# Twelve buffers instead of eight for the gathered rows of the experts, requested nine experts ahead

## The chip, the cores and the metric

The kernel runs on one core of one Trainium2 chip. The metric is device time in microseconds (us) of one execution, as the median of several. The engines of the core are TensorE (PE; its weight loads are listed apart as PEld), VectorE (DVE), ScalarE (ACT), GpSimd (POOL) and SyncE (SP), which here only requests transfers. The transfers run on 16 DMA engines that all queues share.

## What is computed

Four layers in a row, each followed by a layer norm of the residual sum: RWKV attention, a gated feed-forward, latent attention, and a mixture of experts. There are 4096 tokens (16 sequences of 256) of width 256. The change lies in the last layer:

```python
# 32 experts, capacity C = ceil(1.25 * 4096 / 32) = 160 slots each, 4 experts per token
Xp = x[slots_token].reshape(E, C, d)                   # gathered rows, 160 x 256 per expert
G = jnp.einsum('ecd,edi->eci', Xp, W_gate)             # i = 128
U = jnp.einsum('ecd,edi->eci', Xp, W_up)
Y = jnp.einsum('eci,eid->ecd', jax.nn.silu(G) * U, W_down)
Yf = Y.reshape(EC, d) * slots_w[:, None]
out = jnp.zeros((T, d), x.dtype).at[slots_token].add(Yf)
shared = jax.nn.silu(x @ shared_gate.T) * (x @ shared_up.T) @ shared_down.T
x = _layernorm(x + out + shared)
```

## The kernel before

The first three layers and the routing fill the first 1779 us; the routing has left, in the DRAM tensor `slots`, 160 rows for each expert (256 values of the token, 32 weights, one index: 289 floats). `moe_phase` does the rest. Its first part is a loop over the 32 experts, its second part (the tail) reads the sums back, adds them, norms them and stores the output. The engines run their own instruction streams and meet only at semaphores.

One expert e passes these steps:

- **Rows.** SP requests the 160 rows of e from `slots` into `e_rows[:, e % 8]` (`load_slots`, L2714; 80 partitions, two halves). This buffer is read three times: PE transposes it (`expert_turn`, L3095), ACT takes the slot weights out of it while it copies the result (`copy_y`, L2862), and POOL's additions take the indices out of it. So a buffer is free only when the additions of the expert that held it have landed.
- **Weights.** SP requests the three weight matrices of e (`load_w`, L2707) into a ring of seven. It waits until the weights seven experts back have been used by DVE and PE.
- **Matrix work.** PE transposes the rows two experts ahead (L3095), multiplies by gate and up one expert ahead (`expert_in`, L3109), and multiplies by down for e itself (`expert_out`, L3120). ACT and DVE stand between these steps.
- **Additions.** POOL issues two indirect DMAs for e (`add_rows`, L2776), one for each half of 80 rows, that add the result rows in DRAM. Even experts add into `sums0`, odd ones into `sums1`. Two experts that add into the same tensor may not overlap, so POOL first waits until the additions of e - 2 have landed (`y_added`). Result rows lie in `y_rows`, a ring of eight, which the change leaves as it is.

SP's stream in the loop is, for e = 0 to 31: every fourth expert one tile of `x_rows` for the shared part (`load_x`, L2701), then the weights of e + 7, then the rows of e + 7. The wait in front of these rows is on the additions of e - 1. SP stops at a wait, so whatever stands behind it waits too. The waits of `load_slots`, as they stand before:

```python
if e >= RING:
    sp.wait_ge(e_turned, e - RING + 1)
    for a in range(2):
        sp.wait_ge(y_added[e % RING][a], 16 * (e // RING))
```

Between the experts' steps PE, ACT and DVE also do the shared part for seven tiles of 256 tokens, and three more tiles after the loop. The tail starts with SP's wait for all additions (L2752), after which it requests the sums (L2747).

Of the kernel before, what the change touches and what calls it, by code (L numbers as in the profile page):

```python
# [644 lines left out]
E = 32  # L645
CAP = -(-5 * TOKENS // (4 * E))
CH2 = CAP // 2
SLOTROWS = E * CAP
ROW = D + E + 1
# [1925 lines left out]


RING = 8
WRING = 3
SUMRING = 6
STORE_LAG = SUMRING + 4  # L2580
# [11 lines left out]
def moe_phase(nc, w_experts, x3, slots_dram, sums_dram, out, ident, q_rows, wq_high, raw_kept, first_slots):  # L2592
    with ExitStack() as ctx:
        s = Scope(nc, ctx, "moe")

        def both(name, shape):
            return [s.sb(name + "_high", shape, F32R), s.sb(name + "_low", shape, F32R)]
# [6 lines left out]
        h_part = both("h", [P, SC, UNIT])  # L2604
        total = s.sb("total", [P, UT * LATE, D])
        wd_part = both("wd", [P, WRING, D])
        e_rows = s.sb("e_rows", [CH2, RING, 2, ROW])
        e_cols = s.sb("e_cols", [P, 2, KD, CAP])
        e_gate = s.sb("e_gate", [P, 2, CAP])
        e_hidden = s.sb("e_hidden", [P, 2, CAP])  # L2610
        eh_part = both("eh", [P, 2, CAP])
        y_rows = s.sb("y_rows", [CH2, RING, 2, D])
        y_in = s.sb("y_in", [P, SUMRING, SUMS, UT, D])
# [30 lines left out]
        raw_in = [s.sem(f"raw_in{r}") for r in range(WRAW)]  # L2644
        w_high = s.sem("w_high_done")
        w_low = s.sem("w_low_done")
        slots_in = [s.sem(f"slots_in{r}") for r in range(RING)]
        e_turned = s.sem("e_turned")
        e_copied = s.sem("e_copied")
        e_gate_ready = s.sem("e_gate_ready")  # L2650
# [6 lines left out]
        y_copied = s.sem("y_copied")  # L2657
        y_added = [[s.sem(f"y_added{r}_{a}") for a in range(2)] for r in range(RING)]
        sums_in = [s.sem(f"sums_in{r}") for r in range(SUMRING)]
# [14 lines left out]

        def slot_rows(e):

            return first_slots[:, :, :] if e == 0 else e_rows[:, e % RING, :, :]

        def wait_slots(eng, e):

            if e > 0:
                eng.wait_ge(slots_in[e % RING], 16 * (e // RING + (0 if e % RING == 0 else 1)))

        def unit_of(e):

# [11 lines left out]
        def _(sp):  # L2697
            def load_x(u):
                if u >= XRING:
                    sp.wait_ge(total_done, u - XRING + 1)  # L2700
                sp.dma_start(x_rows[:, u % XRING, :, :], unit_rows(x3, EARLY + u)).then_inc(rows_in[u % XRING], 16)  # L2701
# [5 lines left out]
                sp.dma_start(kept_raw(q_rows, raw_kept, e), w_experts[e]).then_inc(raw_in[e % WRAW], 16)  # L2707

            def load_slots(e):
                if e >= RING:  # L2710
                    sp.wait_ge(e_turned, e - RING + 1)
                    for a in range(2):
                        sp.wait_ge(y_added[e % RING][a], 16 * (e // RING))
                sp.dma_start(slot_rows(e),  # L2714
                             slots_dram[e * CAP:(e + 1) * CAP, :].rearrange("(a p) d -> p a d", p=CH2))\
                    .then_inc(slots_in[e % RING], 16)

            load_slots(1)
            load_x(0)
# [10 lines left out]
            load_slots(7)  # L2730
            load_x(2)
            load_x(3)

            for e in range(E):
                u, piece = unit_of(e)
                if piece == 0 and u >= 1 and u - 1 + XRING < LATE:
                    load_x(u - 1 + XRING)
                if e + WRAW < E:
                    load_w(e + WRAW)
                if e >= 1 and e - 1 + RING < E:  # L2740
                    load_slots(e - 1 + RING)

            def load_sums(p):
                if p >= SUMRING:
# [63 lines left out]
        def _(act):  # L2808
# [20 lines left out]
            def weights_high(e):  # L2829
                wait_raw(act, e)  # L2830
                if e >= WRING:
                    act.wait_ge(y_ready, e - WRING + 1)
                nc.scalar.activation(wd_part[0][:, e % WRING, :], kept_raw(q_rows, raw_kept, e)[:, EIN:], ACT.Copy)\
                    .then_inc(w_high, 1)
# [86 lines left out]
        def _(dve):  # L2921
# [24 lines left out]
            def weights_low(e):  # L2946
                dve.wait_ge(w_high, e + 1)
                nc.vector.tensor_tensor(wd_part[1][:, e % WRING, :], kept_raw(q_rows, raw_kept, e)[:, EIN:],
                                        wd_part[0][:, e % WRING, :].bitcast(F32), ALU.subtract).then_inc(w_low, 1)

# [339 lines left out]
```

## Time and profile before

| | us |
|---|---|
| median of 3 runs (1964.30 to 1968.96) | 1964.71 |
| the profiled execution's own time | 1963.74 |
| its span (first to last instruction) | 1961.8 |
| start of the expert loop's first additions | 1787.46 |
| last addition issued | 1912.55 |

All starts are microseconds from the start of the span. The profile names the releaser of an idle engine by the semaphore event that came last before the engine went on; where an instruction waits for several semaphores this can be another one than the one that really held it. The issue of an indirect DMA is an instruction on POOL of about 1.4 us; its transfers end later, and the trace shows that end as the moment at which a waiter goes on.

### The profile page before, as it was taken

What the parts mean: (1) busy time and instruction counts of PE and PEld (TensorE: products, weight loads), DVE (VectorE), ACT (ScalarE), POOL (GpSimd) and SP (SyncE); (2) the same over time, 40 slices, a digit from 0 to 9 for tenths busy, and PEclk for the clock granted to TensorE, in tenths of its full rate; (3) what the DMA queues carried; (4) which work ended last, traced back from release to release, by engine and by line L of the source; (5) the groups of instructions that cost most, each with busy time, mean ns of one, the idle gap of its engine ahead of it and who ended that gap; (6) DMA issues with size and microseconds to landing.
All of it is one profiled execution on the core that took longest, in us unless ns stands there. A gap on an engine that the chain in (4) does not pass through costs nothing. (4 is left out here: it accounts for less than half of the span.)

```text
span 1961.8 us, 35601 instructions
## 1 busy us (share of the span) xinstructions
PE 1833.9 (93%) x12032; PEld 1643.8 (84%) x12032; DVE 1483.0 (76%) x4074; ACT 1039.5 (53%) x2694; POOL 836.0 (43%) x863
## 2 busy tenths in 40 slices
PE   7999999999999999999999999999999999978880
PEld 6788888888888887888789999999999999977870
DVE  7978787787878796656677888888888888863436
ACT  5434343333333333333477777777777777735653
POOL 1232323232323220000244566666666666754776
PEclk9999999999999999999999999999999999988995
DMA  3201010000101003473200010000000000127867
GB/s 121 95 1 33 1 33 23 12 22 12 33 1 50 30 22 120 139 264 127 93 12 18 21 41 26 22 21 20 19 19 20 19 19 14 40 75 186 198 141 260
DMA packets 102003, 118.81 MB, mean 61 GB/s; under 512 B 12567, under 2 KB 93723, under 8 KB 101184
## 3 DMA queue, kind: packets, MB, share of 16 engines
q1 hardware_dynamic: 89104, 108.42, 17.0%
q0 software_dynamic: 12288, 8.11, 2.7%
q8 instruction: 98, 1.61, 0.4%
q14 instruction: 81, 0.66, 0.1%
q10 hardware_dynamic: 432, 0.02, 0.0%
HBM read 75.50 MB, written 57.10 MB: 68 GB/s over the span
## 5 line engine op out<-in xcount | busy, mean ns | idle before, releaser
L282 POOL TENSOR_TENSOR kept_q_rows<-kept_q_rows 128x512 f32<-128x512 f32 x128 | 203.5, 1590 | 527.3 <-DVE kept_q_rows L547 527.3
L1716 POOL TENSOR_TENSOR kept_raw<-kept_raw,mla_row_inv 128x512 f32<-128x512 f32 x192 | 199.2, 1038 | 258.4 <-DVE mla_row_inv L2056 257.2
L372 ACT ACTIVATE kept_q_rows<-rwkv_r 128x512 f32<-128x512 f32 x128 | 76.6, 599 | 399.3 <-DVE rwkv_o_low L468 396.7
L1874 ACT ACTIVATE kept_raw<-kept_raw,mla_least 128x256 f32<-128x256 f32 (+1 forms) x512 | 227.7, 446 | 74.2 <-DVE mla_least L2040 71.7
L2040 DVE CUSTOM_DVE_ANT_0 kept_raw<-mla_score,kept_mask 128x256 f32<-128x256 f32 (+1 forms) x512 | 157.1, 352 | 82.7 <-PE mla_score L2412 52.5
L532 DVE TENSOR_TENSOR kept_q_rows<-rwkv_v,kept_q_rows 128x512 f32<-128x512 f32 x128 | 88.1, 688 | 113.2 <-PE rwkv_v L583 110.9
L539 DVE TENSOR_TENSOR_SCAN rwkv_state<-rwkv_decay_w,kept_q_rows 128x256 f32<-128x256 f32 x256 | 166.0, 691 | 4.1
L1799 POOL DMA_INDIRECT slots<-mla_x_out,mla_slot_now x128 | 130.6, 1020 | 30.8 <-issue 23.2
L1890 ACT ACTIVATE mla_p_high<-mla_turn 128x512 fp32r<-128x512 f32 x192 | 114.0, 594 | 48.1 <-PE mla_turn L2420 46.5
L2050 DVE TENSOR_TENSOR mla_p_low<-mla_turn,mla_p_high 128x512 fp32r<-128x512 f32 x192 | 128.1, 667 | 2.1 <-ACT mla_p_high L1890 2.1
L2420 PE MATMUL mla_turn<-kept_ident,kept_raw 128*128 128x128 f32 x768 | 116.1, 274 | 8.5 <-DVE mla_p_low L2050 8.5
L2439 PE MATMUL mla_o<-mla_p_high,mla_v_high 128*128 128x256 f32 x384 | 117.9, 307 | 0.7 <-DVE mla_o_low L2061 0.4
L2420 PEld LDWEIGHTS mla_turn<-kept_ident,kept_raw 128*128 128x128 f32 x768 | 92.0, 141 | 29.9 <-issue 15.3
L2439 PE MATMUL mla_o<-mla_p_high,mla_v_low 128*128 128x256 f32 x384 | 108.7, 283 | 0.0
L2439 PE MATMUL mla_o<-mla_p_low,mla_v_high 128*128 128x256 f32 x384 | 108.3, 282 | 0.0
L600 PE MATMUL rwkv_out<-rwkv_w_high,rwkv_o_high 128*128 128x256 f32 x352 | 98.8, 281 | 4.8 <-DVE rwkv_o_low L468 4.8
L2776 POOL DMA_INDIRECT sums<-moe_y_rows,moe_e_rows x62 | 88.3, 1424 | 34.9 <-issue 14.3
L2375 PE MATMUL mla_proj<-kept_wq_high,kept_cq_high 128*128 128x512 f32 x240 | 99.0, 412 | 2.2 <-ACT kept_q_rows L1852 1.1
L932 ACT ACTIVATE ffn_gate<-ffn_gate,kept_scale_hid 128x512 f32<-128x512 f32 (+1 forms) x48 | 33.0, 688 | 126.3 <-PE ffn_gate L1164 126.3
L547 DVE SCALAR_TENSOR_TENSOR kept_q_rows<-kept_q_rows,rwkv_bonus_u,rwkv_state 128x512 f32<-128x512 f32 x128 | 96.3, 752 | 4.5
L600 PE MATMUL rwkv_out<-rwkv_w_high,rwkv_o_low 128*128 128x256 f32 x352 | 99.3, 282 | 0.0
L600 PE MATMUL rwkv_out<-rwkv_w_low,rwkv_o_high 128*128 128x256 f32 x352 | 98.6, 280 | 0.0
(505 smaller groups left out, 6265.6 us busy)
## 6 DMA issues: line engine op xcount, KB each, us to landing
kept_raw<-in_experts SPq DMA_DIRECT2D x27, 384.0 KB
kept_raw<-in_rkvo SPq DMA_DIRECT2D x16, 512.0 KB
moe_y_in<-sums SPq DMA_DIRECT2D x32, 256.0 KB, 4.7
sums<-ffn_empty SPq DMA_DIRECT2D x12, 512.0 KB
slots<-ffn_empty SPq DMA_DIRECT2D x16, 361.2 KB
moe_e_rows<-slots SPq DMA_DIRECT2D x31, 180.6 KB
kept_x_in<-x SPq DMA_DIRECT2D x18, 256.0 KB, 17.0
mla_x_res<-x SPq DMA_DIRECT2D x17, 256.0 KB
```

The source lines that it names most:

```text
L282: nc.gpsimd.tensor_tensor(gate[:, c % 2, :], key[:, c % 2, :], gate[:, c % 2, :], ALU.mult).then_inc(gated_done, 1)
L539: last_scan = nc.vector.tensor_tensor_scan(out=state[:, q, 1:SEQ + 1], data0=decay_w[:, c:c + 1].to_broadcast([P, SEQ]), data1=kv[:, q * S ...
L600: last = nc.tensor.matmul(out_ps[j // 2][:, (j % 2) * D:(j % 2 + 1) * D], o_part[op][:, c % 2, j * P:(j + 1) * P], w_chunk(wp, c)[:, 3 * D ...
L1716: nc.gpsimd.tensor_tensor(unit, unit, row_inv[:, v % PR, 0:len(heads)].rearrange("p (h a) -> p h a", a=1) .to_broadcast([P, len(heads), ke ...
L1799: nc.gpsimd.indirect_dma_start(slots_dram, bass.IndirectOffsetOnAxis(slot_now[:, of % 2, i:i + 1], 0), x_out[:, of % 2, i // TOPK, :], Non ...
L1874: last = nc.scalar.activation(probs[:, v % PR, i * keys:(i + 1) * keys], masked[:, v % 2, i * keys:(i + 1) * keys], ACT.Exp, bias=least[:, ...
L1890: nc.scalar.activation(p_part[0][:, v % PR, :], turn_ps[n % TURN_BANKS][:, :], ACT.Copy)\
L2040: last = nc.vector.tensor_tensor_reduce(out=masked[:, v % 2, i * keys:(i + 1) * keys], in0=score_ps[v % 2][:, i * keys:(i + 1) * keys], in ...
L2050: nc.vector.tensor_tensor(p_part[1][:, v % PR, :], turn_ps[n % TURN_BANKS][:, :], p_part[0][:, v % PR, :].bitcast(F32), ALU.subtract).then ...
L2375: last = nc.tensor.matmul(ps[:, :], cp, wp, start=(i == 0), stop=(i == 4))
L2420: last = nc.tensor.transpose(ps[:, i * P:(i + 1) * P], probs[:, v % PR, i * P:(i + 1) * P], ident[:, :])
L2439: last = nc.tensor.matmul(out, v_part[vp][:, seq % 2, kb, b, :], probs_t, start=(i == 0), stop=(i == len(terms) - 1))
```

## The change

The rows get twelve buffers (`SRING`) instead of eight, which takes 27.7 KB of a partition instead of 18.5 KB. SP requests the rows of expert 8 ahead of the loop, and in iteration e of the loop the rows of e + 9 (`SRING - SLACK`) instead of e + 7. The buffer of e + 9 is that of e - 3, so the wait in front of the request is on the transposition and the additions of e - 3, where it was on those of e - 1. The weights stay seven ahead, `y_rows` and the semaphores of the additions stay a ring of eight.

```diff
 RING = 8
+SRING = 12
+SLACK = 3
...
-        e_rows = s.sb("e_rows", [CH2, RING, 2, ROW])
+        e_rows = s.sb("e_rows", [CH2, SRING, 2, ROW])
...
-        slots_in = [s.sem(f"slots_in{r}") for r in range(RING)]
+        slots_in = [s.sem(f"slots_in{r}") for r in range(SRING)]
...
-            return first_slots[:, :, :] if e == 0 else e_rows[:, e % RING, :, :]
+            return first_slots[:, :, :] if e == 0 else e_rows[:, e % SRING, :, :]
...
-                eng.wait_ge(slots_in[e % RING], 16 * (e // RING + (0 if e % RING == 0 else 1)))
+                eng.wait_ge(slots_in[e % SRING], 16 * (e // SRING + (0 if e % SRING == 0 else 1)))
...
             def load_slots(e):
-                if e >= RING:
-                    sp.wait_ge(e_turned, e - RING + 1)
+                if e >= SRING:
+                    sp.wait_ge(e_turned, e - SRING + 1)
                     for a in range(2):
-                        sp.wait_ge(y_added[e % RING][a], 16 * (e // RING))
+                        sp.wait_ge(y_added[(e - SRING) % RING][a], 16 * ((e - SRING) // RING + 1))
...
             load_x(2)
             load_x(3)
+            load_slots(8)
...
-                if e >= 1 and e - 1 + RING < E:
-                    load_slots(e - 1 + RING)
+                if 8 <= e + SRING - SLACK < E:
+                    load_slots(e + SRING - SLACK)
```

No instruction is added or taken away on any engine; only SP's stream has another order. At the start of the expert loop SP's stream before was (rows of 6, weights of 6, rows of 7, two tiles of x, weights of 7 and 8, rows of 8, weights of 9):

```order
L2714 DMA moe_e_rows<-slots 80x2x289
L2707 DMA kept_raw<-in_experts 128x768
L2714 DMA moe_e_rows<-slots 80x2x289
L2701 DMA moe_x_rows<-x3 128x2x256 x2
L2707 DMA kept_q_rows<-in_experts 128x768
L2707 DMA kept_raw<-in_experts 128x768
L2714 DMA moe_e_rows<-slots 80x2x289
L2707 DMA kept_raw<-in_experts 128x768
```

and is now (rows of 6, weights of 6, rows of 7, two tiles of x, rows of 8, weights of 7, rows of 9, weights of 8, rows of 10, weights of 9):

```order
L2716 DMA moe_e_rows<-slots 80x2x289
L2709 DMA kept_raw<-in_experts 128x768
L2716 DMA moe_e_rows<-slots 80x2x289
L2703 DMA moe_x_rows<-x3 128x2x256 x2
L2716 DMA moe_e_rows<-slots 80x2x289
L2709 DMA kept_q_rows<-in_experts 128x768
L2716 DMA moe_e_rows<-slots 80x2x289
L2709 DMA kept_raw<-in_experts 128x768
L2716 DMA moe_e_rows<-slots 80x2x289
L2709 DMA kept_raw<-in_experts 128x768
```

The rows of 8 stood behind the weights of 8 and behind a wait; now the rows of 8, 9, 10 and 11 have no wait on additions at all, and the first such wait (on expert 0) stands in front of the rows of 12.

At the end of the loop SP's stream before was (rows of 29, weights of 30, rows of 30, last tile of x, weights of 31, rows of 31, then the first read of the sums):

```order
L2714 DMA moe_e_rows<-slots 80x2x289
L2707 DMA kept_raw<-in_experts 128x768
L2714 DMA moe_e_rows<-slots 80x2x289
L2701 DMA moe_x_rows<-x3 128x2x256
L2707 DMA kept_raw<-in_experts 128x768
L2714 DMA moe_e_rows<-slots 80x2x289
L2747 DMA moe_y_in<-sums0 128x2x256
```

and is now (rows of 30, weights of 29, rows of 31, weights of 30, last tile of x, weights of 31, then the first read of the sums):

```order
L2716 DMA moe_e_rows<-slots 80x2x289
L2709 DMA kept_raw<-in_experts 128x768
L2716 DMA moe_e_rows<-slots 80x2x289
L2709 DMA kept_raw<-in_experts 128x768
L2703 DMA moe_x_rows<-x3 128x2x256
L2709 DMA kept_raw<-in_experts 128x768
L2750 DMA moe_y_in<-sums0 128x2x256
```

The last request with a wait on additions was for the rows of 31 (on expert 23); now it is again for the rows of 31, but on expert 19, and nothing behind it waits for additions until the sums are read.

## Rows read from the trace of the kernel before

**Rows 1.** The page: the chain that ended last, its shares by engine

```profile
DMA 3%; PE 2%; issue 2%; DVE 1%; POOL 1%; ACT 0%; POOLq 0%; ACTq 0%; DVEq 0%; SPq 0%
```

**Rows 2.** Stretches: us, busy us by engine, clock, DMA share, GB/s

```profile
1780.00:1800.00 20.00, 19.37 (x147) 18.77 (x147) 8.62 (x22) 12.59 (x35) 7.53 (x6) 0.87 0.98 274
1794.00:1796.00 2.00, 2.00 (x19) 2.00 (x18) 1.58 (x4) 1.28 (x5) 1.41 (x1) 1.00 1.12 336
```

**Rows 3.** POOL in order of time: start, us, [idle before, releaser]

```profile
1789.30 1.44 POOL L2776 DMA_INDIRECT sums<-moe_y_rows,kept_first_slots  x1 [0.30 <-issue]
1794.42 1.41 POOL L2776 DMA_INDIRECT sums<-moe_y_rows,moe_e_rows  x1 [3.68 <-ACT moe_y_rows L2862]
1802.96 1.39 POOL L2776 DMA_INDIRECT sums<-moe_y_rows,moe_e_rows  x1 [1.91 <-ACT moe_y_rows L2862]
1811.57 1.39 POOL L2776 DMA_INDIRECT sums<-moe_y_rows,moe_e_rows  x1 [2.11 <-DMA sums<-moe_y_rows,moe_e_rows]
1828.11 1.40 POOL L2776 DMA_INDIRECT sums<-moe_y_rows,moe_e_rows  x1 [2.18 <-DMA sums<-moe_y_rows,moe_e_rows]
1844.30 1.40 POOL L2776 DMA_INDIRECT sums<-moe_y_rows,moe_e_rows  x1 [1.41 <-DMA sums<-moe_y_rows,moe_e_rows]
1873.71 1.55 POOL L2776 DMA_INDIRECT sums<-moe_y_rows,moe_e_rows  x1 [0.30 <-issue]
1886.59 1.40 POOL L2776 DMA_INDIRECT sums<-moe_y_rows,moe_e_rows  x1 [0.91 <-ACT moe_y_rows L2862]
1889.99 1.40 POOL L2776 DMA_INDIRECT sums<-moe_y_rows,moe_e_rows  x1 [0.30 <-issue]
1912.55 1.40 POOL L2776 DMA_INDIRECT sums<-moe_y_rows,moe_e_rows  x1 [0.30 <-issue]
```

**Rows 4.** ACT in order of time: the copy of expert 3's result

```profile
1798.45 0.83 ACT L2862 ACTIVATE moe_y_rows<-moe_y,moe_e_rows 80x256 f32<-80x256 f32 x2
```

**Rows 5.** The chain that ended last, in order of time: start, us, what

```profile
1804.66 6.05 DMA sums<-moe_y_rows,moe_e_rows
1891.69 3.18 DMA sums<-moe_y_rows,moe_e_rows
```

**Rows 6.** SP's requests in order of time: start, us, line, what

```profile
1796.71 0.33 SPq L2714 DMA_DIRECT2D moe_e_rows<-slots  x1
1802.18 0.33 SPq L2714 DMA_DIRECT2D moe_e_rows<-slots  x1
1810.79 0.32 SPq L2714 DMA_DIRECT2D moe_e_rows<-slots  x1
1811.70 0.37 SPq L2714 DMA_DIRECT2D moe_e_rows<-slots  x1
1871.28 0.32 SPq L2714 DMA_DIRECT2D moe_e_rows<-slots  x1
1887.55 0.32 SPq L2714 DMA_DIRECT2D moe_e_rows<-slots  x1
1915.81 2.42 SPq L2747 DMA_DIRECT2D moe_y_in<-sums  x5
```

**Rows 7.** Who waited for whom: us in total, times, longest us

```profile
SPq L2713 <- DMA sums<-moe_y_rows,moe_e_rows: 61.2, 13, 6.4
PEld moe_et L3095 <- DMA moe_e_rows<-slots: 13.3, 12, 2.1
```

**Rows 8.** PE in order of time: transpositions of the rows of experts 6, 14, 31

```profile
1798.26 0.44 PE L3095 MATMUL moe_et<-kept_ident,moe_e_rows 80*128 80x80 f32 x4
1824.46 0.44 PE L3095 MATMUL moe_et<-kept_ident,moe_e_rows 80*128 80x80 f32 x4
1892.03 0.50 PE L3095 MATMUL moe_et<-kept_ident,moe_e_rows 80*128 80x80 f32 x4 [0.94 <-DMA moe_e_rows<-slots]
```

**Rows 9.** Size of one request: out<-in, queue, count, KB

```profile
kept_raw<-in_experts SPq DMA_DIRECT2D x27, 384.0 KB
moe_e_rows<-slots SPq DMA_DIRECT2D x31, 180.6 KB
```

More of the change, by code:

```diff
@@ L2709, in load_slots @@
             def load_slots(e):
-                if e >= RING:
-                    sp.wait_ge(e_turned, e - RING + 1)
+                if e >= SRING:
+                    sp.wait_ge(e_turned, e - SRING + 1)
                     for a in range(2):
-                        sp.wait_ge(y_added[e % RING][a], 16 * (e // RING))
+                        sp.wait_ge(y_added[(e - SRING) % RING][a], 16 * ((e - SRING) // RING + 1))
                 sp.dma_start(slot_rows(e),
                              slots_dram[e * CAP:(e + 1) * CAP, :].rearrange("(a p) d -> p a d", p=CH2))\
-                    .then_inc(slots_in[e % RING], 16)
+                    .then_inc(slots_in[e % SRING], 16)
             load_slots(1)
```

## The prediction, made before the kernel was run

> **What bounds the kernel now.** I read four views, in this order. First the chain of waits that ended last, where DMA has the largest share [rows 1]: in the stretch that the change touches it runs through the indirect additions, their issue on POOL and their landing. Its pieces show an addition that takes 6.05 us from the start of its issue to its landing in the middle of the loop, and 3.18 us near its end [rows 5]. Second the timeline of POOL [rows 3]. Two halves make an expert, so in the loop the rows shown are the first half of expert 1 (1794.42), 3 (1802.96), 5 (1811.57), 9 (1828.11), 13 (1844.30), 21 (1873.71), 24 (1886.59) and 25 (1889.99), and the second half of 0 (1789.30) and of 31 (1912.55). Where POOL has no wait, an issue takes 1.40 us and the gap behind it 0.30 us, so the floor is 1.70 us for a half and 3.40 us for an expert. From the first half of expert 3 to the second half of expert 31 there are 57 steps: 57 x 1.70 = 96.9 us, and the trace shows 1912.55 - 1802.96 = 109.6 us. So 12.7 us of this stretch are waits, and this is all that a change in the loop can give back on this chain, since the tail starts with the landing of the last addition (SP's read of the sums at 1915.81 [rows 6], 3.26 us after 1912.55).
>
> What are these waits? The view names DMA for some and ACT's copy for others [rows 3]. I take the landing of the addition two experts back for all of them from expert 3 on. For expert 3, ACT has finished its copy at 1798.45 + 0.83 = 1799.28 [rows 4], 3.7 us before POOL goes on. And SP, which waits for the additions of expert 1 in front of the rows of expert 9, goes on at 1802.18 [rows 6], 0.78 us before POOL. At expert 5 the same distance stands again: SP at 1810.79 on the landing of expert 3, POOL at 1811.57, again 0.78 us [rows 3, 6]. One landing releases both.
>
> Third, SP's requests [rows 6] and the views of waits [rows 7]. SP waits 61.2 us for additions in front of rows (L2713, 13 times), and PE waits for rows 12 times, 13.3 us by its weight loads. PE's own pace shows how much that is: between the transpositions for experts 6 and 14 there are eight iterations in 26.20 us, 3.275 us each, without a wait; from 14 to 31 there are seventeen in 67.57 us, where 17 x 3.275 = 55.7 us would do. PE loses 11.9 us to late rows [rows 8]. Fourth, the stretches: the DMA engines are busy 0.98 of the time from 1780 to 1800 [rows 2].
>
> **What the change does to PE.** No instruction goes or comes. Rows of expert k + 8 were requested when the additions of k landed; now rows of k + 12. SP's next request, the weights, stands behind that wait: it was k + 9, now k + 11. Rows are used two iterations ahead of their expert, so they come four iterations, some 13 us, earlier than they did, against a longest wait of 2.1 us [rows 7, 8]. So PE's 11.9 us go. What is late next for PE is nothing until its lead over POOL grows: it then meets the weights, that still follow additions, and the eight buffers of `y_rows`. Is it worth anything for the end? POOL needs a result at least 3.40 us after the last one, and from expert 3 on no wait of POOL was for a result. PE earlier is cover on top of cover. I count 0 us.
>
> **What it does to the additions.** This decides, and it has three places.
>
> (a) *The start.* Rows of 8 to 11 and weights 9 and 10 now go out before the landing of expert 0 at about 1796.7, when they did not: 4 x 180.6 + 2 x 384 = 1490 KB [rows 9], at 274 GB/s [rows 2] an estimate of 5.6 us of DMA time, put into a stretch in which the engines are full (share 1.12 in 1794 to 1796 [rows 2]). Expert 0's second half, issued among the first requests, took 1796.7 - 1789.3 = 7.4 us to land; expert 1's, issued at about 1794.42 + 1.70 = 1796.1 when the queue was shorter, 6.0 us [rows 3, 6]. Now expert 1 has the long queue too: between 6.0 and 7.4 us, so expert 3 starts 0 to 1.4 us later. A gain is excluded, as no load is taken away ahead of it. The value lies between two rows that are alike near, and I take the middle, +0.7 us. The weights of 7 and 8 move behind one and two requests of rows (0.7 to 1.3 us each way at that rate), but are used five iterations later: 0.
>
> The Trainium skill (DMA: Bandwidth & Descriptors, section on queues, rings and completion order) states that each DMA engine goes round-robin between the queues it has work for, a packet at a time. By that rule the length of SP's queue would not matter to an addition so long as it is not empty, term (a) would be 0 and the sum 0.7 us lower. The two landings, 7.4 and 6.0 us, both with full engines, differ, so the trace doesn't quite bear it out; the queue's other contents differ too, so it doesn't refute it either.
>
> (b) *The middle.* Here lies the point of the whole change: SP still waits for an addition in every iteration, only for an older one. Is that wait still last? The weights of k + 11 need PE's work on k + 4. Expert 3 lands at 1810.7 while PE has transposed for expert 9 at about 1798.26 + 3 x 3.275 = 1808.1, so it has finished the gate and up work of 7; and PE only gets further ahead. So every landing still lets out one request of rows and one of weights, 565 KB [rows 9], about 2 us at 274 GB/s, at the very moment at which POOL issues the next addition. Two experts that land within 1 us (SP at 1810.79 and again at 1811.70) still let out a double load. The pace in fours of experts has been 16.5, 16.2 and 14.7 us (5 to 9, 9 to 13, and the mean of the two from 13 to 21) [rows 3], against a floor of 13.6 us; this pattern is one of POOL, SP and the DMA engines, and all three see the same bytes in the same order, shifted. The x tile moves from the landing of experts 2, 6, 10 to that of 4, 8, 12: same size, same frequency. I count 0, with bounds from the paces seen: sixteen experts at 14.7 throughout would give -(62.1 - 58.8) = -3.3 us, at 16.5 throughout +3.9 us.
>
> (c) *The end.* Before, the last request goes out at 1887.55 on the landing of expert 23, and from expert 25 on the pace is the floor [rows 3, 6]. Now the last one hangs on expert 19, whose landing is at about 1871.2 [rows 6]. Four experts fewer issue among loads. The least it gives is the wait of expert 24, 0.91 - 0.30 = 0.6 us. The average of waits is 12.7 us over the 22 experts 3 to 24, 0.58 each, so four are worth 2.3 us. Against that, the landing of 19 lets out rows, two weights and a tile of x at once, that is more than the pair before. I take half, -1.2 us, bounds -0.6 and -2.3.
>
> **The sum.** +0.7 + 0 + 0 - 1.2 = -0.5 us on the profiled execution of 1963.74 us: 1963.2 us. The median of the runs shown is 1964.71 us, 1.0 us above it, so the forecast for the median is 1964.2 us. The measurement of this kernel can tell about 0.3%, 5.9 us, from no change; this is within it.
>
> **Rivals.**
> - *Late results do hold POOL.* If the view's label is right where it names ACT's copy, and the chain really passes PE's late rows, PE's 11.9 us come off the end, bounded by POOL's 12.7 us: 1964.7 - 11.9 = 1952.8 us. For it: PE waits 12 times and the chain does contain rows. Against it: the two times of 0.78 us and the copy that was long done. The Trainium skill (DMA: Bandwidth & Descriptors, rules for kernel authors) advises to issue a DMA early and wait on its semaphore late; that rule would promise this rival, and for PE the trace agrees with it, but PE is not what ends last. Chance 0.07.
> - *The bursts fall apart.* If, with SP less tight, requests spread between additions, the middle runs at 14.7 us per four experts (-3.3 us) and the end gives its full 2.3 us, with (a) at 0: 1964.7 - 5.6 = 1959.1 us; at a still better pace of 14.2 another 2 us, 1957. For it: the pace did improve to 14.7 by itself from expert 13 on. Against it: SP's release by landings stays. Chance 0.25, and in a little over half of it the gain is over 5.9 us.
> - *Slower: the early backlog and the worst lock.* If the loads put ahead keep additions at 7.4 us past expert 3 (1.4 us at expert 3, the same again at expert 5) and the pace then locks at 16.5 us for all sixteen experts (+3.9 us), without a gain at the end, it is +6.7 us: 1971.4 us. It decides from the point at which a landing takes 1.35 us longer than the 6.05 us of now. For it: DMA share 0.98 at the start. Against it: these loads then aren't there later. Chance 0.10.
> - *The change doesn't do what it says*, rows come no earlier, since SP's wait is still on additions: then PE still loses its 11.9 us, and the time is the same, 1964.7 us. Since even this gives no change, it lies in the forecast's band. Chance 0.03.
>
> **How the numbers follow.** The forecast, within 4 us of 1964.2, has 0.55; 0.07, 0.25, 0.10 and 0.03 stand above. Over 0.3% faster: 0.07 + 0.14 = 0.21, to which I add 0.03 for gains of the forecast's own mechanism beyond its bounds: 0.24. Slower: 0.10 + 0.02 = 0.12. Within: 0.64. The range reaches down to 1957.0 us, which takes in the fallen bursts and leaves out late results, and up to 1970.0 us, the sum of the upper bounds (+1.4 + 3.9 - 0.6 = 4.7 us, 1969.4 us) and a little of the slower rival.
>
> **What would show it.** In the profile of the changed kernel PE's waits for rows should be nearly gone and its transposition for expert 31 well before 1885; SP should still wait for additions for tens of us at L2715; POOL should hold 10 to 14 us of waits between expert 3 and 31, with landings of about 6 us that follow SP's bursts; from about expert 23 on its pace should be 3.40 us. I am wrong in (b) if fours of experts take under 14.3 us or over 16.5 us on the mean, in (a) if expert 3 starts outside 1802.9 to 1804.5, and wrong about the bound if POOL starts within 1 us after a copy of ACT's again and again.

## The result and the profile after

The changed kernel takes 1969.17 us (median of 20 runs) where the kernel before takes 1964.76 us (20 runs beside them). The ratio is 1.0021 with a 95% interval of 1.0014 to 1.0028: it is 2.8 to 5.5 us slower. In two further comparisons the ratio was 1.0021 (1.0010 to 1.0031) and 1.0014 (1.0005 to 1.0023). The forecast was 0.5 us faster, 1964.2 us. The time lies in the forecast's range, but it moved the other way, and clear of the scatter.

The profiled execution has a span of 1969.0 us. First what the change was made for: the waits of PE and SP in the changed kernel (engine, line waited for, us in total, times, longest).

```profile
PEld moe_et L3098 <- DMA moe_e_rows<-slots: 0.7, 1, 0.7
POOL sums L2779 <- DMA sums<-moe_y_rows,moe_e_rows: 19.8, 16, 3.2
SPq L2715 <- DMA sums<-moe_y_rows,moe_e_rows: 46.3, 15, 6.4
```

PE's 12 waits for rows [rows 7] have become one. SP still waits for additions in front of the rows (46.3 us, 15 times), and POOL waits for them too. PE's timeline in the changed kernel shows the transposition for expert 31:

```profile
1884.28 0.50 PE L3098 MATMUL moe_et<-kept_ident,moe_e_rows 80*128 80x80 f32 x4 [0.49 <-DMA moe_e_rows<-slots]
1930.45 0.80 PE L3086 MATMUL moe_down_ps<-kept_wq_high,moe_h_high 128*128 128x256 f32 x2 [21.63 <-DVE moe_h_low L2940]
```

SP's first request of the last layer came at 1782.97 here and at 1779.44 before. Counted from it, PE is at expert 31 after 101.3 us where it was there after 112.6 us [rows 8]: 11.3 us earlier. What it gained it idles away later: the wait that ends at 1930.45 is 21.63 us long, and in the kernel before the same instruction waited 10.26 us, 11.4 us less:

```profile
1922.67 0.80 PE L3083 MATMUL moe_down_ps<-kept_wq_high,moe_h_high 128*128 128x256 f32 x2 [10.26 <-DVE moe_h_low L2937]
```

The next two fences show POOL and then SP in order of time in the changed kernel, as [rows 3] and [rows 6] do for before.

```profile
1799.72 1.40 POOL L2779 DMA_INDIRECT sums<-moe_y_rows,moe_e_rows  x1 [0.30 <-issue]
...
1807.86 1.39 POOL L2779 DMA_INDIRECT sums<-moe_y_rows,moe_e_rows  x1 [3.22 <-DMA sums<-moe_y_rows,moe_e_rows]
1809.56 1.75 POOL L2779 DMA_INDIRECT sums<-moe_y_rows,moe_e_rows  x1 [0.30 <-issue]
...
1816.95 1.42 POOL L2779 DMA_INDIRECT sums<-moe_y_rows,moe_e_rows  x1 [2.24 <-DMA sums<-moe_y_rows,moe_e_rows]
...
1882.36 1.40 POOL L2779 DMA_INDIRECT sums<-moe_y_rows,moe_e_rows  x1 [2.27 <-DMA sums<-moe_y_rows,moe_e_rows]
...
1890.47 1.39 POOL L2779 DMA_INDIRECT sums<-moe_y_rows,moe_e_rows  x1 [1.45 <-DMA sums<-moe_y_rows,moe_e_rows]
...
1919.37 1.40 POOL L2779 DMA_INDIRECT sums<-moe_y_rows,moe_e_rows  x1 [0.30 <-issue]
```

```profile
1782.97 0.32 SPq L2716 DMA_DIRECT2D moe_e_rows<-slots  x1
...
1807.08 0.31 SPq L2716 DMA_DIRECT2D moe_e_rows<-slots  x1
...
1816.17 0.32 SPq L2716 DMA_DIRECT2D moe_e_rows<-slots  x1
...
1882.96 0.42 SPq L2709 DMA_DIRECT2D kept_raw<-in_experts  x1
1922.65 2.42 SPq L2750 DMA_DIRECT2D moe_y_in<-sums  x5
```

Read them so. Expert 1's second half is issued at 1799.72; its landing lets SP go on at 1807.08 and POOL, with expert 3, 0.78 us later at 1807.86. That landing took 7.4 us, where it had taken 6.0 us. Expert 3's second half, issued at 1809.56, lands at 1816.1, after 6.6 us, and POOL starts expert 5 at 1816.95, again 0.78 us behind SP. The last row with a wait is that of expert 23 (1890.47); from there POOL runs at its floor.

The stretches of both kernels (us, busy us by engine, clock, DMA share, GB/s) show the loads that moved, first of the kernel before:

```profile
1800.00:1820.00 20.00, 20.00 (x173) 20.00 (x172) 9.84 (x24) 14.54 (x40) 13.36 (x10) 1.00 0.80 186
1880.00:1900.00 20.00, 16.25 (x133) 15.33 (x132) 7.11 (x19) 13.04 (x36) 15.93 (x12) 1.00 0.72 149
```

and of the changed one:

```profile
1800.00:1820.00 20.00, 20.00 (x173) 20.00 (x172) 9.21 (x23) 15.51 (x44) 12.61 (x9) 1.00 0.99 265
1880.00:1900.00 20.00, 14.46 (x107) 12.60 (x105) 6.18 (x15) 9.69 (x29) 13.85 (x11) 1.00 0.56 104
```

The DMA engines are now full from 1800 to 1820, and emptier than before at the end. The changed profile's last layer begins 3.5 us later, so the two stretches don't hold quite the same work. Counted from SP's first request they say the same in all profiles of the two kernels (three of before, four of the changed one, below): from 20 to 30 us after it the share is 0.86 to 0.90 before and 1.09 to 1.10 in the changed kernel, from 95 to 110 us after it 0.83 to 0.85 before and 0.60 to 0.67 in the changed kernel.

One profile can't settle 4 us, since the loop scatters by some us from one execution to the next. So I cut it into three stretches, in every profile at the same rows: from SP's first request of the last layer to the first addition of expert 5, from there to that of expert 21, and from there to the last addition of expert 31. For the changed kernel above: 1816.95 - 1782.97 = 34.0, 1882.36 - 1816.95 = 65.4, and 1919.37 - 1882.36 = 37.0 us.

| us | to expert 5 | 5 to 21 | 21 to the last | together |
|---|---|---|---|---|
| before, three profiles | 32.1, 29.8, 31.9 | 62.1, 64.1, 62.0 | 38.8, 38.3, 38.8 | 133.1, 132.2, 132.6 |
| changed, four profiles | 34.0, 34.6, 35.2, 34.2 | 65.4, 60.4, 62.5, 62.8 | 37.0, 36.5, 37.8, 37.5 | 136.4, 131.5, 135.6, 134.6 |
| difference of the means | +3.2 | +0.1 | -1.4 | +1.9 |

(The second profile of before is the kernel that only allocates the buffers, below. Without it the start would be 2.5 us later in the changed kernel and not 3.2, the middle 0.7 us, the end -1.6 us, the whole +1.7 us.)

The landing at which the start parts can be read in every profile too: from the issue of expert 1's second half to SP's next request on it took 6.0, 4.6 and 6.5 us before, and 7.4, 7.6, 7.9 and 7.2 us in the changed kernel. Expert 3's, in the same way, took 6.1, 5.0 and 5.2 us before and 6.6, 7.0, 7.3 and 7.0 us after. The tail, from the last addition to the end of the span, took 49.2 to 50.0 us in both. SP's first request came at 1779.4, 1779.2 and 1780.9 before and at 1783.0, 1782.3, 1779.1 and 1781.1 in the changed kernel; in the nine other kernels of this study (ten profiles), whose streams up to there are the same, it came at 1777.4 to 1782.9. I take that for scatter of the layers ahead.

### The profile page after: what moved, and what is told of

The parts are those of the page before. It is cut to its first block and busy times, and to the rows that moved or that the text cites. A ratio compares the mean times of both kernels' runs of the same rounds, so it can differ in the third digit from the quotient of the medians.

```text
span 1969.0 us, 35597 instructions
## 1 busy us (share of the span) xinstructions
PE 1836.9 (93%) x12032; PEld 1648.6 (84%) x12032; DVE 1483.4 (75%) x4074; ACT 1037.9 (53%) x2694; POOL 834.9 (42%) x863
## 5 line engine op out<-in xcount | busy, mean ns | idle before, releaser
L2779 POOL DMA_INDIRECT sums<-moe_y_rows,moe_e_rows x62 | 88.0, 1420 | 38.3 <-DMA sums<-moe_y_rows,moe_e_rows 19.8
```

The lines of the kernel that those rows point to most:

```text
L2779: nc.gpsimd.indirect_dma_start(sums_dram[e % SUMS], bass.IndirectOffsetOnAxis(slot_rows(e)[:, a, IDCOL:ROW].bitcast(U32), 0), y_rows[:, e ...
```

## The experiments

Theory S (in the first four texts it is still called Q, the loop's queue) says that the loss arises in the start: rows of 8 to 11 and weights of 9 and 10 (1490 KB) now compete with the first additions, and the end gives back less than this costs. Its rivals: L, the layout alone costs; M, the loss arises in the middle of the loop, since SP runs ahead of the additions there; and B, that SP's bursts decide, so that another distance helps.

### Only the buffers

```diff
-        e_rows = s.sb("e_rows", [CH2, RING, 2, ROW])
+        e_rows = s.sb("e_rows", [CH2, 12, 2, ROW])
-        slots_in = [... for r in range(RING)]
+        slots_in = [... for r in range(12)]
```

> The kernel before with the twelve buffers and twelve semaphores of the rows only allocated: it still uses eight of them, in the order of before. Theory L (layout): the other places of tiles and semaphores cost something by themselves, since the changed kernel's last layer began 3.5 us later (SP's first request at 1782.97 against 1779.44); then this kernel is 2 to 4 us slower than before. Theory Q (the loop's queue): the loss lies in the loop, and the late begin is scatter between executions; then this kernel is within 1 us of before and expert 3's first addition starts 23.5 us after SP's first request (1802.96 - 1779.44), as before.

Measured: ratio 0.9999 (0.9989 to 1.0010). SP's first request came at 1779.24, and expert 3 started 22.3 us after it. The layout costs nothing that can be seen; theory L falls.

### The changed kernel again

> The changed kernel once more, beside the others on one chip. Its ratio should be 1.0014 to 1.0028 again. Theory L: SP's first request of the last layer is again near 1783. Theory Q: it is anywhere between 1779 and 1783, and the stretch from it to the last addition is again about 136.4 us (1919.37 - 1782.97), where before it was 133.1 us (1912.55 - 1779.44).

Measured: ratio 1.0021 (1.0010 to 1.0031). SP's first request came at 1782.31, but the loop took 131.5 us, not 136.4: in this one profile it is as short as before, while the runs beside it are 2.0 to 6.1 us slower. Its start is late all the same (POOL in order of time: expert 3, expert 5):

```profile
1807.39 1.40 POOL L2779 DMA_INDIRECT sums<-moe_y_rows,moe_e_rows  x1 [3.42 <-DMA sums<-moe_y_rows,moe_e_rows]
...
1816.88 1.40 POOL L2779 DMA_INDIRECT sums<-moe_y_rows,moe_e_rows  x1 [2.84 <-DMA sums<-moe_y_rows,moe_e_rows]
```

That is 25.1 and 34.6 us after the first request. The start is steady from profile to profile, the middle is not. I expected the whole to repeat, which was wrong.

### Other distances

Seven ahead, waiting five back:

```diff
-SLACK = 3
+SLACK = 5
-            load_slots(8)
```

> Twelve buffers, but rows requested seven experts ahead as before, so the wait is on the additions of the expert five back instead of one back; no rows of 8 ahead of the loop. Theory Q, as a theory of the start's backlog: rows of 8 to 10 no longer go out among the first requests, but weights 9 and 10 still do, since SP does not stop; expert 3 starts 0.3 to 1.0 us later than before, the whole is 0 to 2 us slower than before. Rival B (bursts that coincide with the additions): SP is now led by PE's work, not by landings, so requests fall apart; POOL's waits from expert 3 on shrink from 12.7 us to under 9 us and the kernel is 3 to 5 us faster than before.

Measured: ratio 1.0014 (1.0003 to 1.0026). The stretches are 34.8, 62.9 and 35.8 us. The whole is 0.6 to 5.1 us slower than before. Without a wait on recent additions SP asks for rows 8 and on, and for weights, as fast as PE lets it, and the start is as late as in the changed kernel. My number for its start was too small (expert 3 at 25.2 us against 22.3 to 24.3 in the kernels before, not 0.3 to 1.0 us later). Rival B, which promised 3 to 5 us from looser bursts, falls.

Eleven ahead, waiting one back:

```diff
-SLACK = 3
+SLACK = 1
-            load_slots(8)
+            for n in range(8, SRING - SLACK):
+                load_slots(n)
```

> Twelve buffers, rows requested eleven experts ahead, the wait on the additions of the expert one back as before; rows of 8, 9 and 10 go out ahead of the loop. The weights again follow the landings as before (k + 9 on the landing of k). Theory Q: what counts is how much is requested before expert 1's additions: 4 x 180.6 KB of rows instead of the changed kernel's rows and weights, so expert 3 is 0.7 to 1.4 us late and the kernel 1 to 4 us slower than before. If instead the weights that run ahead are what costs, expert 3 is under 0.5 us late and the kernel within 1.5 us of before.

Measured: ratio 1.0033 (1.0019 to 1.0046), the slowest of all; stretches 35.3, 61.2 and 39.2 us, expert 3 at 25.9 us. Here the weights follow the landings as before and only rows come early. So weights that run ahead are not needed for the late start; my numbers for it (expert 3 late by 0.7 to 1.4 us, the whole by 1 to 4 us) were too small, since expert 3 is 2.5 us later than the mean of before and the whole 3.7 to 9.0 us slower. The end shows no gain, although SP's last request goes out as early as in the changed kernel (98 us after its first, there 100 us, before 108 us). The last rows hang on expert 19, and when it lands SP requests at once all that is left, 181 KB of rows, four weights and a tile of x (1973 KB). SP in order of time, and under it POOL at expert 23:

```profile
1876.40 0.32 SPq L2716 DMA_DIRECT2D moe_e_rows<-slots  x1
1876.81 0.40 SPq L2709 DMA_DIRECT2D kept_q_rows<-in_experts  x1
1877.30 0.86 SPq L2709 DMA_DIRECT2D kept_raw<-in_experts  x2
...
1878.73 0.42 SPq L2709 DMA_DIRECT2D kept_raw<-in_experts  x1
```

```profile
1887.33 1.53 POOL L2780 DMA_INDIRECT sums<-moe_y_rows,moe_e_rows  x1 [3.48 <-DMA sums<-moe_y_rows,moe_e_rows]
```

Expert 21's second half, issued at 1878.88 into this burst, took 7.7 us to land (1887.33 - 0.78 - 1878.88), and the wait for it eats the gain.

### The start of before, the lead later

```diff
-            load_slots(8)
...
-                if 8 <= e + SRING - SLACK < E:
-                    load_slots(e + SRING - SLACK)
+                if 1 <= e <= 8:
+                    load_slots(e + 7, old=True)      # waits for expert e - 1
+                elif e in (9, 10):
+                    load_slots(2 * e - 2)
+                    load_slots(2 * e - 1)
+                elif 11 <= e and e + 9 < E:
+                    load_slots(e + 9)
```

> The changed kernel with the start of before: rows up to expert 15 are requested seven ahead and wait for the additions of the expert one back; then SP requests the rows of two experts in each of iterations 9 and 10 and goes on as the changed kernel does, nine ahead and three back. Theory S (the start's backlog): the changed kernel loses 1.4 to 3 us at experts 3 to 5 by what it requests ahead of the first landings; this one starts expert 5's additions 30 to 32.5 us after SP's first request, as before, and is within 1.5 us of the kernel before. Theory M (loads and additions lock in the middle, wherever the start is): the middle costs 2 us or more, so this one is 2 to 4 us slower than before in spite of its start.

Measured: ratio 1.0016 (1.0006 to 1.0027). The start is that of before (31.8 us), the end has the gain (36.8 us), but the middle takes 68.8 us. SP in order of time, where it catches up, and under it POOL at experts 9, 11 and 13:

```profile
1825.95 0.32 SPq L2719 DMA_DIRECT2D moe_e_rows<-slots  x1
1826.37 0.40 SPq L2709 DMA_DIRECT2D kept_raw<-in_experts  x1
1826.86 0.86 SPq L2719 DMA_DIRECT2D moe_e_rows<-slots  x2
1827.81 0.39 SPq L2709 DMA_DIRECT2D kept_raw<-in_experts  x1
1828.31 0.92 SPq L2719 DMA_DIRECT2D moe_e_rows<-slots  x2
```

```profile
1826.74 1.39 POOL L2786 DMA_INDIRECT sums<-moe_y_rows,moe_e_rows  x1 [2.86 <-DMA sums<-moe_y_rows,moe_e_rows]
...
1837.69 1.39 POOL L2786 DMA_INDIRECT sums<-moe_y_rows,moe_e_rows  x1 [4.41 <-ACT moe_y_rows L2872]
...
1846.14 1.55 POOL L2786 DMA_INDIRECT sums<-moe_y_rows,moe_e_rows  x1 [1.96 <-DMA sums<-moe_y_rows,moe_e_rows]
```

From 9 to 13 POOL takes 19.4 us, where the slowest four experts of before took 16.5 us [rows 3] and no other kernel of this study took more than 16.9 us there. Within some 3 us SP lets out the rows of five experts and two weights, and by 1832 the rows of another, two more weights and a tile of x. Expert 9's second half, issued at 1828.44, takes 8.5 us to land: SP, whose next request of rows waits for it too, goes on at 1836.90, again 0.79 us before POOL (the label ACT in POOL's row names a copy that was done before). So the cost comes back where the lead is taken, and the start is no special place; its size there rests on one profile. The whole is 1.2 to 5.3 us slower. That is what theory M had forecast (2 to 4 us), and theory S as I had put it (within 1.5 us of before) doesn't hold for this kernel. M's reason, that loads and additions lock in the middle wherever the start is, isn't what the rows show: the delay sits at the burst.

### Bytes added in the start

Rows of 8 to 11 loaded once more, ahead of the loop, into buffers that nothing reads; the rest is the kernel before:

```diff
             load_x(3)
+            for n in range(8, 12):
+                sp.dma_start(e_rows[:, n, :, :], slots_dram[n * CAP:(n + 1) * CAP, :]...)
```

> The kernel before, with the rows of experts 8 to 11 loaded once more ahead of the loop, behind the tiles of x, into four buffers that nothing reads: 722 KB more in the start and no other difference. Theory S: expert 3's additions start 24.5 to 26 us after SP's first request instead of 22.3 to 23.5, and the kernel is 1.5 to 4 us slower than before. Theory M: the start's loss is absorbed by less waiting behind it, the kernel is under 1 us slower.

Measured: ratio 1.0016 (1.0007 to 1.0025), 1.4 to 4.9 us slower. Expert 3 starts 25.1 us after the first request (POOL in order of time):

```profile
1802.53 1.40 POOL L2782 DMA_INDIRECT sums<-moe_y_rows,moe_e_rows  x1 [3.45 <-DMA sums<-moe_y_rows,moe_e_rows]
```

with the first request at 1777.44. 722 KB of loads with no other effect make expert 3 as late as the change does; the landing of expert 1 takes 7.6 us here. Expert 5 follows at 33.2 us, later than before (29.8 to 32.1) but not as late as in the changed kernel (34.0 to 35.2). The other stretches are 64.6 and 36.9 us. This kernel has all of its loads at the end, and its end is as short as the changed kernel's: a single profile can't show a term of 1 to 2 us there.

All six requests of the changed kernel once more, at its places (with a spare tile for the weights):

> The kernel before, with all six requests that the changed kernel puts ahead of expert 0's landing (rows of 8 to 11, weights 9 and 10) made once more at the changed kernel's places, into buffers that nothing reads: 1490 KB more in the start, the stream of before behind it. Theory S: this is the changed kernel's loss without its gain at the end; expert 5's additions start 33.5 to 35.5 us after SP's first request (changed kernel 34.0 and 34.6, before 32.1 and 29.8) and the kernel is 4 to 7 us slower than before. Theory M (the loss of the changed kernel arises in the middle, the start's is absorbed behind it): under 2.5 us slower.

Measured: ratio 1.0013 (1.0004 to 1.0022), 0.8 to 4.3 us; stretches 34.7, 63.4 and 37.3 us. The start is as late as expected, but in this profile expert 0 itself came 1.2 us later than elsewhere, and 33.5 us are left without that. The landing of expert 1 takes 7.6 us, as with 722 KB, that of expert 3 5.7 us, where the changed kernel has 6.6 to 7.3 us. So the added loads reproduce the first late landing in full, and the second only in part. The loss is smaller than the 4 to 7 us that I expected: it is not more than that of 722 KB.

### Bytes taken away

Two tiles of x (512 KB) moved out of the start, behind the rows of 8 and 12:

```diff
-            load_x(2)
-            load_x(3)
...
+                if e in (1, 5):
+                    load_x(2 + e // 4)
```

> The kernel before with two tiles of x (256 KB each) moved out of the requests ahead of the loop, to behind the rows of experts 8 and 12. Theory S: 512 KB less in the start let expert 1 land earlier; expert 3's additions start 21.9 to 22.8 us after SP's first request and the kernel is 0 to 2 us faster than before. Theory M: the same bytes come back in the middle, and the kernel is within 0.7 us of before.

Measured: ratio 1.0010 (1.0001 to 1.0019), 0.2 to 3.7 us slower. Both forecasts miss. Expert 3 starts at 22.5 us, at the early side of what the kernels before show (22.3 to 24.3), and the stretches are 31.2, 65.3 and 39.4 us: no gain is left at expert 5, and the 512 KB come back behind it. The hope to gain by a lighter start falls, which also speaks against theory S in its simple form.

Weights of experts 10 to 31 left out (8448 KB less):

```diff
-                sp.dma_start(kept_raw(q_rows, raw_kept, e), w_experts[e])...
+                if e < 10:
+                    sp.dma_start(kept_raw(q_rows, raw_kept, e), w_experts[e])...
```

> The kernel before, which leaves out the loads of the weights of experts 10 to 31 (22 x 384 KB; they compute with the weights seven experts back); the rest is as it was. It prices what loads beside the additions cost in all. If POOL's waits from expert 3 on (12.7 us) come from loads that slow the additions, they fall under 4 us and the kernel is 8 to 11 us faster than before. If additions take their 6 us by themselves when they follow each other, the waits stay above 9 us and the kernel is under 3 us faster.

Measured: ratio 0.9960 (0.9945 to 0.9974), 5.1 to 10.8 us faster. POOL's waits for additions, in the view of waits:

```profile
POOL sums L2777 <- DMA sums<-moe_y_rows,moe_e_rows: 2.4, 6, 0.9
```

From expert 3 to the end there are 2.4 us of waits where there were 12.7. (The other two profiles of before have 13.0 and 11.5 us.) Loads beside the additions are the cause of these waits, about (12.7 - 2.4) / 8.448 = 1.2 us for each MB, as a mean over the loop.

The last rows (28 to 31) and weights (30, 31) left out, 1490 KB, which is what the changed kernel takes out of the end:

```diff
-                sp.dma_start(slot_rows(e), ...)
+                if e < 28:
+                    sp.dma_start(slot_rows(e), ...)
```

> The kernel before, which leaves out the last loads that the changed kernel moves forward: rows of experts 28 to 31 and weights of 30 and 31 (they compute with what the buffers hold): 1490 KB less in the end, everything else as before. It measures the most that the changed kernel can get back there. By the forecast's term for the end and by the two changed profiles (21's first to 31's last addition 37.0 and 36.5 us against 38.8 and 38.3) it is 1.2 to 2.5 us faster than before. Theory S wants this to be less than what the start costs. If it is 4 us or more, start and end would cancel and the loss of the changed kernel would have to lie in the middle (theory M).

> The kernel before without the loads of the rows of experts 28 to 31 and of weights 30 and 31, once more, beside the light start on one chip. Both theories: 0 to 3 us faster than before, as in its first run.

Measured: ratio 0.9992 (0.9983 to 1.0000) and 0.9998 (0.9989 to 1.0007). The end takes 37.2 and 38.2 us. So the most to be had there is 0 to 3.3 us by the one run and at most 2.2 us by the other. I had expected 1.2 to 2.5 us, later 0 to 3. By the means of the table the changed kernel took 1.4 us of it. Beside the first of these runs, on the same chip, stood the kernel with all six requests added; it is 4.5 us slower than this one (3.2 to 5.7).

### Running ahead without the early bytes

The changed kernel, but of the rows of 8 to 11 only 33 columns are loaded (PE transposes expert 0's in their place), and weights 9 and 10 are left out:

```diff
+                at = D if 8 <= e < 12 else 0
-                sp.dma_start(slot_rows(e), ...)
+                sp.dma_start(slot_rows(e)[:, :, at:ROW], ...)
...
+                if e not in (9, 10):
                     sp.dma_start(kept_raw(q_rows, raw_kept, e), w_experts[e])...
```

> The changed kernel with a light start: of the rows of experts 8 to 11 only the 33 last columns (weights and index, 21 KB each) are loaded, and weights 9 and 10 are left out, so these experts compute with expert 0's rows and with the weights of 2 and 3. That is about 1400 KB less ahead of the first landings; from there on SP runs nine ahead and waits three back as the changed kernel does. Theory S: expert 5's additions start 30 to 32.5 us after SP's first request, the end keeps its gain (21's first to 31's last addition 36 to 37.8 us), and the kernel is 0.5 to 2.5 us faster than before, as the kernel with the same bytes left out at the end. Theory M: the middle costs 2 us or more by running ahead, and it is 0 to 2 us slower than before.

> The changed kernel once more on the same chip: 2.5 to 5.5 us slower than before. A fourth profile of its stages: 34 to 35.5 us to expert 5's additions, 60 to 65.5 us from there to 21's, 36.5 to 38 us to the last. Theory M would need the middle stretch above the 62.0 to 64.1 us of the kernel before.

Measured on one chip: the light start 1.0004 (0.9993 to 1.0014), the changed kernel 1.0014 (1.0005 to 1.0023), the kernel with the light end 0.9998 (0.9989 to 1.0007). Stretches of the light start: 31.0, 61.8 and 38.5 us. POOL in order of time, experts 3 and 5, with SP's first request at 1778.77:

```profile
1801.40 1.39 POOL L2782 DMA_INDIRECT sums<-moe_y_rows,moe_e_rows  x1 [0.76 <-issue]
...
1809.74 1.40 POOL L2782 DMA_INDIRECT sums<-moe_y_rows,moe_e_rows  x1 [0.30 <-issue]
```

With the 1400 KB gone from the start, expert 1 lands in 4.9 us and the start is that of before, although SP runs nine ahead through all of the loop. The middle (61.8 us) shows no cost of a lead that is kept; it is one profile, of an execution (1961.69 us) near the fastest of its eleven, and the middle scatters from 60.4 to 65.4 us among the kernels here (the one with the late catch-up aside). The run-time comparison is weak. The light start is not clear of the light end (which theory S wants equal) nor of the changed kernel (2.0 us faster on the mean, with an interval from 0 to 4.1), and it isn't faster than before, as I had expected.

### A third look at both

> The kernel before once more, for a third profile of its stages beside the others on one chip. Theory S: expert 5's additions start 29.8 to 32.5 us after SP's first request; from there to expert 21's 60 to 65 us; from 21's first to 31's last addition 38 to 39 us. SP's first request falls anywhere between 1777 and 1783 us, as scatter of the layers ahead.

> The changed kernel once more, for a third profile of its stages on the same chip. Theory S: expert 5's additions start 33.5 to 35 us after SP's first request; from there to expert 21's 60 to 65 us as in the kernel before; from 21's first to 31's last addition 36 to 37.2 us. Theory M: the stretch from 5 to 21 is over 66 us again.

Measured: 31.9, 62.0 and 38.8 us for before; 35.2, 62.5 and 37.8 us for the changed kernel. They are the third values of the table's first two rows. Before came as expected. In the changed kernel the middle did; the start is 0.2 us and the end 0.6 us above what I had given.

## Why the prediction was wrong

**What bounds the kernel: right.** The 0.78 us between SP and POOL stands in the changed kernel twice more, and the kernel without most weights turns 12.7 us of waits into 2.4 us. PE's lateness was worth nothing: PE came 11.3 us earlier (11.9 forecast) and the end did not move forward. POOL's waits on additions are still there (14.6, 9.5, 13.3 and 13.0 us from expert 3 on in the four profiles, 12.7, 13.0 and 11.5 us before). The first rival, in which late rows hold POOL, falls with that. With it goes what the Trainium skill's rule (DMA: Bandwidth & Descriptors, rules for kernel authors: issue early, wait late) would have promised: it held for PE's wait and not for the kernel, since the DMA issued early slowed another one that the end hung on.

**(b) The middle, 0: not contradicted.** The mean of the four profiles is 0.1 us above the mean of the three, but the four run from 60.4 to 65.4 us, so a term of 1 or 2 us could hide there. SP's 15 waits on additions show that landings still lead it.

**(c) The end, -1.2: right in size, as far as it can be told.** The mean is -1.4 us, with the four profiles at 36.5 to 37.8 and the three at 38.3 to 38.8 us, and the kernels that leave the same bytes out bound it at 0 to -3.3. Against too much trust in it: two kernels with all their loads at the end took 36.9 and 37.3 us, and the light start took 38.5 us.

**(a) The start, +0.7: here it failed.** I had the cause, and bounds of 0 to 1.4 us by two landings of 6.0 and 7.4 us, and took the middle of them though all requests put ahead fall into a stretch with full engines. The landing took 7.2 to 7.9 us in the four profiles, the upper end and a little more: expert 3 starts 1.7 us later (25.0 against 23.4 us, means of four and three). The lower bound, 6.0 us, was one reading of a landing that takes 4.6 to 6.5 us before. And I ended the term at expert 3. The load was still there when expert 3's additions were issued (DMA share 0.99 from 1800 to 1820 against 0.80), so expert 5 was late a second time, by 1.5 us more: +3.2 us together, against the +0.7 of the sum. I had written that second step down as part of the slower rival, and gave it 0.10. The slower rival as a whole (1971.4 us, with a pace of 16.5 us in the middle) did not come; its first half did. My sign of being wrong stopped at expert 3 as well: counted from SP's first request its limits are 23.5 and 25.1 us, and the mean of 25.0 us lies inside, just.

The round-robin rule that I had weighed beside (a) (the Trainium skill, DMA: Bandwidth & Descriptors, queues, rings and completion order) would have made the term 0. The term isn't 0, but that does not refute the rule. As I had put it, it needs a queue that is never empty, and I took the engines as full during both landings of the kernel before. For expert 1's they were not: the DMA share is 0.96 over its 6.05 us and 0.80 in the last 2 us, where the changed kernel has 1.08 and 1.10. And expert 0's second half took 7.4 us in all three profiles of before and 7.4 to 7.7 us in the changed kernel, though there four or five more requests of SP went out while it was under way. That is what the rule would give: a longer queue costs an addition nothing while it lasts, it only lasts longer and so catches the next ones. It isn't proven: the share was also near 1 (1.04) in the profile in which expert 1 landed in 4.6 us, and with the requests eleven ahead expert 1's landing took 8.2 us.

**The sum.** With (a) at +3.2, (b) at +0.1 and (c) at -1.4 the profiles give +1.9 us; the three timed comparisons give +4.1, +4.1 and +2.8 us, with intervals from 1.0 to 6.1. The loop's length scatters in the changed kernel from 131.5 to 136.4 us, so four profiles fit both. What is shown is that the loop's start is late, by 3.2 us on the mean, and that loads beside expert 1's additions do it: added alone they bring the late expert 3 (7.6 us landings) and 1.9 to 2.2 us at expert 5, and without them the start is that of before. What makes the rest of the second step in the changed kernel, about 1 us, isn't shown. Whether a further 1 to 2 us arise somewhere else (in the layers ahead, where the first request came 1.6 us later on the mean, within the scatter of the other kernels, or in the middle) stays open. Open too is why 1490 KB of added loads cost no more than 722 KB; the landing of expert 1 takes 7.6 us with either.

No kernel of this study that computes everything beat the kernel before: the two that are closest are the kernel before with the larger allocation (0.9999) and the one with x moved (1.0010).

## What to carry to other kernels

Before moving loads forward, ask which transfer the end hangs on and whether it shares the engines with them: a load that comes earlier frees the engine that waited for it, but its bytes are paid by the transfers beside it at the new place. Here the engines were full at the new place (share 0.98) and less so at the old one, and the move cost more than it gave. Loads that one landing lets out together can cost as much as an early backlog: bursts behind a single wait gave landings of 7.7 and 8.5 us in two of the kernels. When a term's cause is clear, take the value of the row that is most alike, not the middle, look at more than one profile before a landing is made a bound, and follow the delay to the next step of the chain before closing the term.

## What the runs showed of the hardware

- An indirect addition of 80 rows takes 3.2 us from issue to landing 4 us after SP's last request [rows 5, 6]. Expert 1's second half took 4.6 to 6.5 us in the three profiles of before and 7.2 to 7.9 us in the four of the changed kernel, in which SP's requests filled the whole landing (DMA share 1.08 to 1.09). Expert 0's, issued right behind SP's first requests, took 7.4 to 7.7 us in both. Leaving 8448 KB of weights out took 10.3 of 12.7 us of waits away.
- The same 1490 KB are not worth the same everywhere, by the means of the profiles: +3.2 us in the start (DMA share 0.98), -1.4 us at the end (share 0.72 from 1880 to 1900).
- The time of SP's first request in the last layer differs by up to 5.6 us (1777.4 to 1783.0) between profiles of kernels whose streams up to there are the same.
